# Linear attention's opening: halved first taps and convolutions, and a new order of its first two steps

## The reference

```python
q = silu(causal_dwconv(hidden @ Wq, qconv_w, qconv_b))    # 4 taps along the rows; k in the same way
k = silu(causal_dwconv(hidden @ Wk, kconv_w, kconv_b))
q, k = layernorm(q, qn_w, qn_b), layernorm(k, kn_w, kn_b) # over the 128 of a head
v, gate = hidden @ Wv, silu(hidden @ Wg)
beta = sigmoid(hidden @ Wb + bb)                          # one per row and head
S = (1.0 - b) * S + b * (v_t k_t^T)                       # scan over the rows, per head
o_t = S q_t                                               # then (o * gate) @ Wo
```

## Time and profile before

| | |
|---|---|
| median of 3 runs | 1077.67 us (1076.04 to 1078.31) |
| profiled execution | 1080.33 us, span 1078.4 us |
| mean granted clock of TensorE | 0.978 |
| busy in the span: PE, DVE, ACT, POOL | 95%, 72%, 63%, 46% |
| linear attention's first half projections start | 391.54 us |

### The profile page before, as it was taken

The page is one execution under the profiler, slowest core; times in us unless marked ns, Lnnn a source line. Parts: engine busy times, 40 slices in busy tenths (PEclk is TensorE's granted clock), DMA queues, the critical chain, the costliest instruction groups (busy, mean ns, idle before and its releaser), DMA issues. The chain is left out here.

```text
span 1078.4 us, 19331 instructions
## 1 busy us (share of the span) xinstructions
PE 1026.1 (95%) x6893; PEld 812.2 (75%) x6893; DVE 778.2 (72%) x1645; ACT 676.2 (63%) x1229; POOL 500.4 (46%) x441
## 2 busy tenths in 40 slices
PE   7999999999999996899999999999799999999997
PEld 4333333467888885898899888999699778888997
DVE  5888999546677747889998999989567465333843
ACT  4578888766554447887788787887446344333454
POOL 3350320114069542777767777676406000536643
PEclk9989999999999998899999999999889999999999
DMA  4453443233134203331231122210011123555200
GB/s 100 84 85 49 73 70 58 59 98 98 60 108 111 37 2 107 110 101 64 64 109 64 55 65 82 91 67 23 2 35 33 45 53 94 155 158 156 74 21 20
DMA packets 80795, 79.31 MB, mean 74 GB/s; under 512 B 29385, under 2 KB 67741, under 8 KB 80701
## 3 DMA queue, kind: packets, MB, share of 16 engines
q1 hardware_dynamic: 79968, 77.14, 27.3%
q10 hardware_dynamic: 732, 0.95, 0.3%
HBM read 65.51 MB, written 1.28 MB: 62 GB/s over the span
## 5 line engine op out<-in xcount | busy, mean ns | idle before, releaser
L744 ACT ACTIVATE attn_probs<-attn_rows_k 128x512 f32<-128x512 f32 x256 | 138.9, 595 | 27.9 <-PE attn_rows_k L590 24.7
L590 PE MATMUL attn_rows_k<-attn_q_stack,attn_k_stack 50*128 50x512 f32 x256 | 96.1, 455 | 0.0
L2946 DVE TENSOR_TENSOR late_mids<-late_mids,late_bank 128x512 f32<-128x512 f32 (+1 forms) x50 | 34.4, 687 | 77.8 <-PE late_bank L67 74.8
L603 PE MATMUL attn_ctx<-attn_probs,attn_v 128*32 128x256 f32 x1024 | 83.7, 400 | 1.4
L855 DVE TENSOR_REDUCE attn_row_max<-s_sum 128x1 f32<-128x1024 f32 x62 | 75.6, 1220 | 13.0 <-PE s_sum L574 6.8
L855 DVE TENSOR_REDUCE attn_row_max<-attn_rows_q 128x1 f32<-128x1024 f32 x62 | 75.9, 1224 | 10.1 <-PE attn_rows_q L574 7.3
L65 PE MATMUL late_bank<-net_x_part_low,late_w_T 128*128 128x512 f32 (+1 forms) x192 | 77.9, 405 | 0.0
L66 PE MATMUL late_bank<-net_x_part_low,late_w_T 128*128 128x512 f32 (+1 forms) x192 | 76.1, 396 | 0.0
L67 PE MATMUL late_bank<-net_x_part_low,late_w_T 128*128 128x512 f32 (+1 forms) x192 | 76.1, 396 | 0.0
L2851 ACT ACTIVATE late_mids<-late_bank 128x512 f32<-128x512 f32 (+1 forms) x50 | 29.9, 597 | 69.5 <-PE late_bank L67 69.5
L1611 POOL TENSOR_TENSOR gold_mids<-gold_mids,s_later 128x512 f32<-128x512 f32 x32 | 51.9, 1660 | 45.9 <-DMA s_later<-gold_weights 45.9
(11 more groups left out here) (463 smaller groups left out, 3523.8 us busy)
## 6 DMA issues: line engine op xcount, KB each, us to landing
lin_mix<-decay_sums SPq DMA_DIRECT2D x16, 512.0 KB, 4.2
lin_q_dec<-decay_sums SPq DMA_DIRECT2D x16, 512.0 KB, 5.4
s_later<-gold_weights SPq DMA_DIRECT2D x16, 256.0 KB, 3.6
attn_k_stack<-s_part SPq DMA_DIRECT2D x30, 128.0 KB, 3.5
s_raw_ring<-in_L_ffn_Wg SPq DMA_DIRECT2D x12, 256.0 KB, 2.7
s_raw_ring<-in_L_ffn_Wu SPq DMA_DIRECT2D x12, 256.0 KB, 3.3
attn_k_stack<-s_part SPq DMA_DIRECT2D x33, 64.0 KB, 2.3
gold_raw_w_down<-in_L_ffn_Wd SPq DMA_DIRECT2D x1, 2048.0 KB, 12.3
```

The source lines that it names most:

```text
L590: pe.matmul(out, k_stack[rows, h % SLOTS, t * P:(t + 1) * P], q_stack[rows, h % SLOTS, :], start=True, stop=True).then_inc(scored_k, 1)
L603: i = pe.matmul(sums[j * VW:(j + 1) * VW, :], v[:, t, h, :], probs[:, (2 * w + odd) % PB, j * QUARTER:(j + 1) * QUARTER], start=(t == 0), ...
L744: act.activation(probs[:, (2 * k + odd) % PB, side * HALF:(side + 1) * HALF], ring_bank(("exped", 4 * k + n + 1)), ACT.Exp).then_inc(exped, 1)
```

## The change

Per engine:

- **TensorE.** `pe_first` does q, k, z, v instead of q, z, k, v, and counts the two first halves done. The opening's order is new: q's rows ahead of `project_v(1)`; `sum_decay` between the halves of `project_k(1)`; `turn_q(0)` ahead of `rows_k(0)` and `project_q(1)`, which now waits for q_T of head 0 where `turn_q(0)` waited for the convolution of head 1; the gate of head 0 before head 1's q rows; `project_q(2)` between `score(0)` and `key_values(0)`. The loop starts at step 3.
- **ScalarE.** Two half taps in `act_first`, two half taps in the opening for the second halves; k's silu of head 0 ahead of the exponential; then a new order: q_T of head 0 early, the high parts of v(1), q(2), k(2) and `exp_mix(0)` ahead of head 1's silus, `norm_k(0)` behind them.
- **VectorE.** The convolutions of head 0 are done in halves, the first ones between `dve_shift` and `dve_low` and behind `dve_low`. The logits follow both convolutions of head 0, q's variances go ahead of `decay_logs`, head 1's convolutions are k, q, and ahead of `shift_k(0)`.
- **GpSimd.** The low parts of gate 0, v(1), q(2), k(2), `mask(0)` and `decay_v(0)` go ahead of `power(1, q)`, `k_rows` of head 0 behind it, then `power(1, k)`, and `mask(1)`.
- **SP.** The loads of q(2), k(2), v(1) and gate(1) are issued ahead of the wait for the decay rows.

```diff
@@ -1588,8 +1588,10 @@
             tail1.dve_shift(dve, j)
+        linear.first_half_conv(dve, 0)
         for j in (2, 3):
             tail1.dve_low(dve, j)
+        linear.first_half_conv(dve, 1)
 
@@ -1708,6 +1710,7 @@
         self.q_projected, self.k_projected, self.g_projected, self.v_projected = (sem(f"{m}_projected") for m in "qkgv")
+        self.first_projected, self.first_tapped = sem("first_projected"), sem("first_tapped")
         self.q_tapped, self.k_tapped, self.q_conved, self.k_conved, self.q_acted, self.k_acted = (
@@ -1769,6 +1772,9 @@
         load_gate(0)
+        load_qk(2)
+        load_v(1)
+        load_gate(1)
         sp.wait_ge(self.rows_ready, 1)
@@ -1777,13 +1783,13 @@
                 prefetch(sp)
-            if 2 <= n + 1 < LH:
+            if 3 <= n + 1 < LH:
                 load_qk(n + 1)
...
                 load_mix(n + 1)
-            if n % 2 == 0 and 1 <= n // 2 + 1 < LH // 2:
+            if n % 2 == 0 and 2 <= n // 2 + 1 < LH // 2:
                 load_v(n // 2 + 1)
-            if 1 <= n < LH:
+            if 2 <= n < LH:
                 load_gate(n)
@@ -1815,11 +1821,11 @@
         pe.wait_ge(self.q_split, 1)
-        self.project_half(pe, "q", 0, self.pair[3])
+        self.project_half(pe, "q", 0, self.pair[3]).then_inc(self.first_projected, 1)
+        pe.wait_ge(self.k_split, 1)
+        self.project_half(pe, "k", 0, self.pair[1]).then_inc(self.first_projected, 1)
         pe.wait_ge(self.b_split, 1)
         self.project_z(pe, 0)
-        pe.wait_ge(self.k_split, 1)
-        self.project_half(pe, "k", 0, self.pair[1])
         pe.wait_ge(self.v_split, 1)
@@ -1862,7 +1868,7 @@
             pe.wait_ge(self.q_normed, h + 1)
-            if h + 1 < LH:
+            if 1 <= h < LH - 1:
                 pe.wait_ge(self.q_conved, h + 2)
@@ -1876,16 +1882,21 @@
             pe.wait_ge(self.q_split, h + 1)
+            if h == 1:
+                pe.wait_ge(self.q_T_done, 1)
             pe.wait_ge(self.q_normed, h)
...
 
-        def project_k(h):
+        def project_k(h, between=None):
             pe.wait_ge(self.k_split, h + 1)
...
                 pe.wait_ge(self.k_conved, 1)
-            project("k", pair[1], self.k_projected)
+            self.project_half(pe, "k", 0, pair[1])
+            if between:
+                between()
+            self.project_half(pe, "k", 1, pair[1]).then_inc(self.k_projected, 1)
 
@@ -1950,14 +1961,24 @@
         finish_first()
+        rows_q(0)
         project_v(1)
-        rows_q(0)
-        sum_decay()
-        project_k(1)
+        project_k(1, sum_decay)
+        turn_q(0)
         rows_k(0)
         project_q(1)
-        turn_q(0)
-        for n in self.STEPS[2:LH + 1]:
+        project_gate(0)
+        rows_q(1)
+        turn_k(0)
+        rows_k(1)
+        score(0)
+        project_q(2)
+        key_values(0)
+        project_k(2)
+        project_v(2)
+        turn_q(1)
+        outputs(0)
+        for n in self.STEPS[3:LH + 1]:
             if live(n - 1):
@@ -1986,9 +2007,17 @@
         self.high(act, "q", self.wq[0], self.q_high)
+        self.high(act, "k", self.wk[0], self.k_high)
         self.high(act, "b", self.wb, self.b_high)
-        self.high(act, "k", self.wk[0], self.k_high)
         self.high(act, "v", self.wv[0], self.v_high)
+        for m, pair in enumerate((3, 1)):
+            act.wait_ge(self.first_projected, m + 1)
+            self.first_tap(act, m, pair, 0, self.first_tapped)
+
+    def first_tap(self, act, m, pair, half, done):
+        cols = slice(half * HALF, (half + 1) * HALF)
+        act.activation(self.conv[m][:, cols], self.pair[pair][:, cols], ACT.Identity, scale=self.taps[:, m, 0, TAPS - 1:TAPS],
+                       bias=self.taps[:, m, 0, TAPS:TAPS + 1]).then_inc(done, 1)
 
@@ -2084,32 +2113,41 @@
         live = self.live
-        tap(0, 0, 3, self.q_projected, self.q_rowed, self.q_tapped)
+        act.wait_ge(self.q_projected, 1)
+        self.first_tap(act, 0, 3, 1, self.q_tapped)
         high_q(1)
-        tap(0, 1, 1, self.k_projected, self.k_rowed, self.k_tapped)
+        act.wait_ge(self.k_projected, 1)
+        self.first_tap(act, 1, 1, 1, self.k_tapped)
         high_k(1)
...
         silu(0, 0, self.q_conved, self.q_acted)
+        silu(0, 1, self.k_conved, self.k_acted)
         exp_logit()
...
         decay_rows()
-        silu(0, 1, self.k_conved, self.k_acted)
+        high_gate(0)
+        q_transposed(0)
         tap(1, 1, 1, self.k_projected, self.k_rowed, self.k_tapped)
-        high_gate(0)
+        high_v(1)
         tap(1, 0, 3, self.q_projected, self.q_rowed, self.q_tapped)
+        high_q(2)
+        high_k(2)
+        exp_mix(0)
+        silu(1, 1, self.k_conved, self.k_acted)
+        silu(1, 0, self.q_conved, self.q_acted)
         norm_k(0)
-        silu(1, 0, self.q_conved, self.q_acted)
-        q_transposed(0)
-        silu(1, 1, self.k_conved, self.k_acted)
-        exp_mix(0)
+        silu_gate(0)
+        k_transposed(0)
         for n in self.STEPS[2:LH]:
-            if live(n):
+            if live(n) and n > 2:
                 high_q(n)
-            k_transposed(n - 2)
-            if live(n):
+            if n > 2:
+                k_transposed(n - 2)
+            if live(n) and n > 2:
                 high_k(n)
-            silu_gate(n - 2)
-            if n % 2 == 0 and live(n):
+            if n > 2:
+                silu_gate(n - 2)
+            if n % 2 == 0 and live(n) and n > 2:
                 high_v(n // 2)
@@ -2142,6 +2180,21 @@
 
+    def conv_part(self, dve, h, m, first, last):
+        src = self.pair[(3, 1)[m]]
+        for j in range(TAPS - 1):
+            back = TAPS - 1 - j
+            at = max(first, back)
+            i = dve.scalar_tensor_tensor(self.conv[m][:, at:last], src[:, at - back:last - back], self.taps[:, m, h, j:j + 1],
+                                         self.conv[m][:, at:last], ALU.mult, ALU.add)
+            if j < TAPS - 2:
+                dve.drain()
+        return i
+
+    def first_half_conv(self, dve, m):
+        dve.wait_ge(self.first_tapped, m + 1)
+        self.conv_part(dve, 0, m, 0, HALF)
+
     def dve(self, dve):
@@ -2193,15 +2246,9 @@
 
-        def convolve(h, m, pair, tapped, done):
+        def convolve(h, m, tapped, done):
             dve.wait_ge(tapped, h + 1)
-            for j in range(TAPS - 1):
-                back = TAPS - 1 - j
-                i = dve.scalar_tensor_tensor(self.conv[m][:, back:T], self.pair[pair][:, 0:T - back],
-                                             self.taps[:, m, h, j:j + 1], self.conv[m][:, back:T], ALU.mult, ALU.add)
-                if j < TAPS - 2:
-                    dve.drain()
-            i.then_inc(done, 1)
+            self.conv_part(dve, h, m, HALF if h == 0 else 0, T).then_inc(done, 1)
 
@@ -2231,17 +2278,17 @@
         live = self.live
-        convolve(0, 0, 3, self.q_tapped, self.q_conved)
+        convolve(0, 0, self.q_tapped, self.q_conved)
+        convolve(0, 1, self.k_tapped, self.k_conved)
         logits()
-        convolve(0, 1, 1, self.k_tapped, self.k_conved)
+        variances(0, 0, 3, self.q_rowed, self.q_rstd, self.q_var)
         decay_logs()
-        variances(0, 0, 3, self.q_rowed, self.q_rstd, self.q_var)
+        norm_q(0)
         mix_biases()
-        norm_q(0)
         variances(0, 1, 2, self.k_rowed, self.k_rstd, self.k_var)
+        convolve(1, 1, self.k_tapped, self.k_conved)
+        convolve(1, 0, self.q_tapped, self.q_conved)
         shift_k(0)
-        convolve(1, 0, 3, self.q_tapped, self.q_conved)
-        convolve(1, 1, 1, self.k_tapped, self.k_conved)
         variances(1, 0, 3, self.q_rowed, self.q_rstd, self.q_var)
@@ -2251,8 +2298,8 @@
             if live(n):
-                convolve(n, 0, 3, self.q_tapped, self.q_conved)
-                convolve(n, 1, 1, self.k_tapped, self.k_conved)
+                convolve(n, 0, self.q_tapped, self.q_conved)
+                convolve(n, 1, self.k_tapped, self.k_conved)
             gate(n - 2)
@@ -2324,23 +2371,28 @@
         power(0, 0, self.q_var, self.q_normed, self.q_rstd)
+        low("gate", self.wg[0], self.g_high, self.g_split, 1)
         power(0, 1, self.k_var, self.k_normed, self.k_rstd)
-        low("gate", self.wg[0], self.g_high, self.g_split, 1)
+        mask(0)
+        low("v", self.wv[1], self.v_high, self.v_split, 2)
+        low("q", self.wq[0], self.q_high, self.q_split, 3)
+        low("k", self.wk[0], self.k_high, self.k_split, 3)
+        decay_v(0)
+
+        pool.sem_clear(range(min(used_numbers), max(used_numbers) + 1))
+        power(1, 0, self.q_var, self.q_normed, self.q_rstd)
         rows_k(0)
-        mask(0)
-        power(1, 0, self.q_var, self.q_normed, self.q_rstd)
+        power(1, 1, self.k_var, self.k_normed, self.k_rstd)
         mask(1)
-
-        pool.sem_clear(range(min(used_numbers), max(used_numbers) + 1))
-        decay_v(0)
         for n in self.STEPS[2:LH]:
-            if live(n - 1):
```

(10 more changed lines are left out.)

## The result

The changed kernel takes 1082.11 us in the median of 20 runs, against 1077.07 for 20 runs of the kernel before beside them: ratio 1.0041 [1.003, 1.0053], so slower by 3.2 to 5.7 us, 4.4 in the middle. Ratios here leave out runs in a slower state, of the changed kernel two (1175.06 and 3603.16 us). The forecast was +2.5 us.

The account below looks back on a forecast made before the run. TensorE bounds the repeating heads; the opening holds 11.7 us of gaps and some clock loss. Order +0.8 and clock +1.7 gave +2.5 us: 1082.8 against the profiled execution, 1080.2 against the median; range 1075.6 to 1083.0.

Parts of the forecast that it names:

- a: First q projection of the linear attention to rows_q(1): forecast 41.8 us, before 44.13, so 2.4 shorter.
- b: From rows_q(1) to project_q(2): forecast 11.7 us, before 11.64, so 0.1 longer.
- c: From project_q(2) to outputs(0): forecast 14.1 us, before 9.45, so +4.7.
- The clock term: At project_q(2) and key_values(0): the clock falls in the new gap ahead of them, +1.7 us, bounds 0 and 4.6.
- forecast gap of 3.5 us: TensorE has nothing between score(0) and project_q(2), 441.5 to 445.0, until norm_q(1) ends.
- z's place: z behind both first-half projections: its clock fall meets the values instead of the k half, counted as nothing.
- Halves: Head 0's half convolutions on VectorE: 2.1 us for three; q's delays the second half's value matmuls +0.35 (0.1 to 2.2).
- the term from the rows: ScalarE table load at head 1's silus: 1.28 us, next activation right behind, against the skill's 2.66 with a drain.
- Rival 1: Only the order costs, the clock holds in the 3.5 us gap before project_q(2): +0.8, 1078.5; chance 0.24.
- Rival 2: Faster: mix(0) lands early, in 2.5 instead of 4.0, and the clock is back soon: -2.0, 1075.7; chance 0.14.
- Rival 3: mix(0) lands late, 5.2 to 6.1 instead of 4.0, moving all from mask(0): 1081.4 to 1082.3; chance 0.09.
- Rival 4: The opening doesn't move: the decay chain sets it in both, the clock costs the same: 1077.7; chance 0.13.

Follow-up runs that it names:

- e9: The changed kernel profiled and timed once more, no edit; ratio to the kernel before 1.0050 [1.0029, 1.0072].
- e3: The changed kernel with key_values(0) ahead of project_q(2), as in the kernel before; ratio to the kernel before 0.9985 [0.9959, 1.0011].
- e5: The changed kernel with POOL's k_rows of head 0 ahead of power(1, q) instead of behind it; ratio to the kernel before 1.0027 [1.0005, 1.005].
- e6: The changed kernel with the edits of e3 and e5 together; ratio to the kernel before 1.0013 [0.9993, 1.0033].
- e8: e6 with z again between the q half and the k half; ratio to the kernel before 1.0003 [0.9983, 1.0022].
- e10: The changed kernel with head 0's k_rows on POOL in pieces of 256 columns, four a pass; ratio to the kernel before 1.0031 [1.0, 1.0063].
- e12: The changed kernel with the edits of e10 and e3 together; ratio to the kernel before 1.0024 [1.0009, 1.0039].
- e2: The changed kernel with z again between the q half and the k half; ratio to the kernel before 1.0013 [0.9984, 1.0042].
- e1: The kernel before with only head 0's first taps and convolutions in halves, every other order kept; ratio to the kernel before 1.0002 [0.9975, 1.0028].
- e11: The kernel before profiled once more, one run, no edit; 66.76 us from first q projection to head 0's first outputs matmul.

## Why the prediction was right in direction and low in size

By means of the two profiles of each kernel, a changed by -0.6 (44.17 against 44.73), b by +2.1 (13.88 against 11.83) and c by +4.6 (14.03 against 9.44): +6.1, where the timed runs say 4.4 to 5.4 (3.1 to 7.8 over both intervals). The prediction's instants give -2.4, +0.1 and +4.7, together +2.3 where the sum said +2.5. So the steps that failed are a and b.

- **Part c, right.** key_values(0) "queued behind project_q(2)", states late, conv q(2) late, clock fallen in the new gap. All is there: the states wait 4.69 for TensorE, conv q(2) runs behind them until 458.29, turn_q(1) waits 0.80 for it, and project_q(2) takes 4.18 (445.60 to 449.78) where it was forecast at 2.85 and a clock loss shared with key_values. The clock term was 1.7, measured 1.3, and 1.9 in e9 (4.75 us for project_q(2)). e3 shows the cause: the exchange alone gives 9.71.
- **Part b, missed.** The step from "k's statistics begin 439.8" to norm_q(1)'s end at 445.0 took the small add between them at its 0.17 us. It took 2.22, held by POOL's pass over 1024 columns, and made the forecast gap of 3.5 us 5.53. The same step had put the two k_rows passes beside these statistics and asked only what they do to power(1, k). e5 moves the hold to the other add (e6 and e8 repeat it: q's add 0.71 and 0.70, k's 0.17), and where k's add is short, b is near 12 (e5, e6, e8, e10: 11.87 to 12.09; not in e12, where key_values(0) makes TensorE wait). That it costs time by itself is shown in the stage (b), but not told apart in the timed runs, where e3, with its b of 14.19, is no slower than before.
- **Part a, mis-sized.** "Its clock fall then meets the values instead of the k half, of like size, so I count nothing." In the changed kernel the clock was at 1.2 GHz from about 393.9 to about 404, 10.2 us, where the profile that the prediction had shows two falls of 3.4 us, from 395.2 and from 408.9; the second half's q projection took 2.56 (401.28 to 403.84) where a half at full clock takes 1.41 (six matmuls, 387.31 to 388.72). The sums began 27.54 into the stage (e9: 26.77), where 24.9 was forecast: 2.7 and 1.9 late, and rows_q(1) is late by 2.7 and 2.1. So the whole miss in a stands ahead of the sums; behind them mix's landing (4.0), mask, exp_mix without a table load and the idle of 6.04 (forecast 6.3) are as worked out. It isn't the luck of one execution: up to the sums e3, e6, e10 and e12 are the changed kernel too, and the six profiles have the sums at 26.77 to 29.46, all later than the 24.89 and 26.06 of the kernel before. z's place, the term put at nothing, is a likely part: the second half's q starts 13.97 to 13.99 into the stage in all six, and 12.78 and 12.79 in e2 and e8, with z second (before: 12.28 and 13.44). Against it, e1 has z second and 13.98. How much is z's place and how much the instants of the falls, which every profile has in these first 25 us, stays open.
- **Halves.** q's three half instructions took 2.40, forecast 2.1; the value matmuls of the second half began 11.25 into the stage instead of 10.74: +0.51, forecast +0.35. Right.
- **ScalarE's table.** The load took 1.28 and the silu stands 0.01 behind its end, so the drain that the page ScalarE: Activation LUTs of the Trainium skill adds (What ACT_TABLE_LOAD costs) isn't seen here either; the term from the rows was right.
- **Rivals.** Rival 1 (the clock holds in the gap) is excluded by 0.63 at 445.6 to 449.5 and 0.77 us for the first matmul in both profiles. Rival 2 needed mix(0) to land in 2.5; it took 4.0. Rival 3 needed 5.2 or more. Rival 4 is excluded by c.
- **The range, in part luck.** The measured time lies just over the 1082 that the forecast had as its own end. What reached further was rival 3's late landing (1082.3) and a clock term at its bound of 4.6 (1083.1), and neither came; the held add, which did, was in no term. The end at 1083.0 doesn't follow from the bounds named for it: 1082.3 and a half convolution of 1.28 in place of 0.69 an instruction, three times, make 1084.1.

## What to carry to other kernels

When a matmul group is queued behind another that waits, ask first what the queued one releases: key_values(0) was ready in a gap of idle TensorE, and one exchange of two lines was worth 4.1 us of the stage and, in e3's timed runs, the whole loss. Splitting an operation pays only where its result is what the path waits for next; the same halves were worth nothing measurable in the old order and some 4 us of the stage in the new one. And before a small VectorE instruction that reads and writes SBUF is put on the path, look at what POOL has running at that instant, not only at the queues that wait for one another.

## What the hardware showed that was not expected

**A tiny VectorE instruction is held by a long POOL instruction.** The 128x8 add, with no semaphore between it and POOL's pass, took 2.2 us in the changed kernel, e9 and e3, 1.46 in e11 and 0.72 in e5, where it started inside a pass of POOL over 1024 columns, and ended 0.03 to 0.04 us behind that pass's end; with POOL idle it takes 0.17. The trace shows it as busy time of VectorE, not as a wait, so it is only seen by its duration. The Trainium skill (SBUF — State Buffer, Who interferes with whom) says that VectorE and GpSimd share a pair of SBUF ports by an exclusive lock held for a whole instruction, that a tensor_scalar can be of the kind that needs the pair, and that the second to come fully blocks. For the passes over 1024 columns the trace agrees, down to the instant of release. For POOL's power on 128x8 it doesn't: the same add ran in 0.17 us inside its 1.65 us (e5, and so in e6 and e8). Not every VectorE instruction is held either: in the changed kernel the statistics of k (1.68 us, from PSUM) and their aggregation (0.64 us) ran beside POOL's first pass at the durations that q's have with POOL idle.

**Clock falls under a TensorE that counts as busy** come at instants that vary by execution. In the window 394.5 to 404 of the changed kernel it was busy 7.74 of 9.5 us, at 1.2 GHz throughout; e9 has its falls at other places of the same work. Two windows of the first 100 us, of the kernel before in e11 and of the changed kernel, show how much such a fall moves all that follows:

```profile
0.00:100.00 100.00, 88.73 (x514) 0.88 0.42 79
```

```profile
0.00:100.00 100.00, 88.92 (x607) 1.00 0.43 81
```

The stage began at 399.95 in the first and at 387.31 in the second, and 12.6 us of difference ahead of it say nothing on the change: two profiles are to be compared from a common instant next to the edit.
